# A state-space mixer on one core: chunk output, gate and skip term with channels on the partitions

## What is computed

```
gate, xbc, dt = split(h @ W_in.T)                 # 4096, 4096 + 2*1024, 64
x, B, C = split(silu(causal_conv4(xbc) + conv_b))
dt = softplus(dt + dt_bias);  A_cs = cumsum(dt * -exp(A_log)) within a chunk
Y_diag = ((C @ B.T) * exp(A_cs[l] - A_cs[s]), s <= l) @ (x * dt)
state  = decayed sum over chunks of B.T @ (x * dt * decay)
Y_off  = (C @ state_before) * exp(A_cs)
y   = Y_diag + Y_off + D * x
g   = y * silu(gate)
g   = g * rsqrt(mean over the 512 channels of a group (g*g) + eps) * norm_weight
out = g @ W_out.T
```

## Time and profile before

| | us |
|---|---|
| median of three runs (2715.51 to 2718.09) | 2717.3 |
| span of the profiled execution | 2716.7 |
| busy in it: TensorE matmul / VectorE / ScalarE / GpSimd | 2384.9 / 2075.4 / 1173.9 / 1157.6 |
| mixer's chunk loop, first to last output projection | 297 to 1616 |

### The profile page before, as it was taken

The page is one execution under the profiler, slowest core; times in us unless marked ns, Lnnn a source line. Parts: engine busy times, 40 slices in busy tenths (PEclk is TensorE's granted clock), DMA queues, the critical chain, the costliest instruction groups (busy, mean ns, idle before and its releaser), DMA issues. The chain is left out here.

```text
span 2716.7 us, 41390 instructions
## 1 busy us (share of the span) xinstructions
PE 2384.9 (88%) x14084; PEld 1851.0 (68%) x14084; DVE 2075.4 (76%) x3420; ACT 1173.9 (43%) x2311; POOL 1157.6 (43%) x1249
## 2 busy tenths in 40 slices
PE   4994999999999999999999972799999976888872
PEld 3784788888888888888888851688888864333322
DVE  5876888888888888888888856677777767766635
ACT  1431555555555555555555531122222223554551
POOL 3442565656656566565665540345555420000000
PEclk9996999999999999999999995899999997999996
DMA  2002000000000000000000010100000003111103
GB/s 84 1 13 96 3 3 30 3 29 4 3 30 3 30 3 3 30 3 30 3 3 3 3 57 7 33 26 26 26 26 20 26 20 108 52 50 49 51 34 122
DMA packets 72016, 77.75 MB, mean 29 GB/s; under 512 B 21120, under 2 KB 57312, under 8 KB 70560
## 3 DMA queue, kind: packets, MB, share of 16 engines
q1 hardware_dynamic: 71840, 75.51, 8.5%
HBM read 59.42 MB, written 15.86 MB: 28 GB/s over the span
## 5 line engine op out<-in xcount | busy, mean ns | idle before, releaser
L1043 DVE SCALAR_TENSOR_TENSOR mix_cv<-mix_pp,mix_cw,mix_cv 128x384 f32<-128x384 f32 (+4 forms) x864 | 493.1, 571 | 25.3 <-ACT mix_cv L966 4.5
L890 PEld LDWEIGHTS mix_pyd<-mix_xdt,mix_lm 128*128 128x128 f32 x2048 | 248.7, 193 | 56.7 <-issue 53.1
L1726 DVE TENSOR_REDUCE att_tops<-att_psc 128x1 f32<-128x512 f32 (+3 forms) x384 | 193.7, 552 | 104.9 <-PE att_psc L1677 72.0
L966 ACT ACTIVATE mix_cv<-mix_pp,mix_cb,mix_cw 128x384 f32<-128x384 f32 (+1 forms) x288 | 182.1, 632 | 210.7 <-PE mix_pp L77 210.7
L75 PE MATMUL mix_pp<-l0in_XH,mix_wx_lo 128*128 128x384 f32 (+2 forms) x576 | 239.0, 415 | 38.1 <-DVE mix_ss L1032 23.1
L829 POOL TENSOR_TENSOR mix_xdt<-mix_xtok,l_dt 128x512 f32<-128x512 f32 x128 | 133.5, 1043 | 279.2 <-ACT mix_xtok L993 279.2
L1202 POOL TENSOR_TENSOR ffn_hl<-ffn_h,ffn_hh 128x512 fp32r<-128x512 f32 x112 | 144.3, 1289 | 251.5 <-ACT ffn_hh L1260 251.5
L941 PE MATMUL mix_pgt<-mix_wo,mix_gt 128*128 128x256 f32 x1024 | 246.6, 384 | 2.9 <-issue 2.2
L890 PE MATMUL mix_pyd<-mix_xdt,mix_lm 128*128 128x64 f32 x2048 | 244.0, 273 | 2.6 <-DVE mix_lm L1093 2.6
L822 POOL TENSOR_TENSOR mix_t<-mix_t,mix_xd 128x512 f32<-128x512 f32 x112 | 144.3, 1288 | 219.6 <-DVE mix_t L1057 128.6
L1750 ACT ACTIVATE att_pr<-att_pst 128x1024 f32<-128x1024 f32 (+7 forms) x256 | 157.8, 651 | 153.9 <-PE att_pst L1688 79.5
(11 more groups left out here) (337 smaller groups left out, 6723.9 us busy)
## 6 DMA issues: line engine op xcount, KB each, us to landing
mix_w_raw<-in_w_in SPq DMA_DIRECT2D x8, 1280.0 KB, 5.7
ffn_raw<-in_wgu SPq DMA_DIRECT2D x56, 128.0 KB, 2.2
mix_ll<-cs SPq DMA_DIRECT2D x384, 4.0 KB
a_part<-att_sums SPq DMA_DIRECT2D x128, 34.0 KB
mix_wo_raw<-in_w_out SPq DMA_DIRECT2D x8, 512.0 KB, 6.7
ffn_draw<-in_wd SPq DMA_DIRECT2D x28, 128.0 KB, 2.1
q<-qkv_part SPq DMA_DIRECT2D x24, 128.0 KB, 1.9
k<-qkv_part SPq DMA_DIRECT2D x24, 128.0 KB, 1.9
```

Source lines behind the costliest of these rows:

```text
L890: last = pe.matmul(pyd[:, h * HP:(h + 1) * HP], lm[p % 2][:, h, :], xdt[p % 2][:, h * HP:(h + 1) * HP], start=True, stop=True)
L966: act.activation(conv_tile(k), pp[k % 2][:, halo:cols], ACT.Identity, bias=cb[:, it // 2, ct:ct + 1], scale=cw[:, it // 2, ct, 3:4]).then_ ...
L1043: last = dve.scalar_tensor_tensor(out, of, cw[:, g, ct, 3 - d:4 - d], out, ALU.mult, ALU.add)
L1726: dve.tensor_reduce(tops[o][:, col:col + 1], psc[PLACE[n, g] % RING][:, 0:end - c], AX.X, ALU.max).then_inc(mx_done, 1)
```

## The change

The chunk output is computed transposed. For each pair of heads, one head's 64 channels go to partitions 0 to 63 of the bank `py` and the other's to 64 to 127. The factor exp(A_cs), which varies along the tokens and so no longer lies on the partitions, comes from DRAM: `prelude` stores it, SyncE loads it for every chunk broadcast over the partitions (512 KB), and GpSimd multiplies it by C (`ce`). The state's part is then accumulated in PSUM by TensorE. The gate is projected with channels on the partitions, two channel tiles for two chunks at a time, one chunk ahead, and kept in SBUF (`sg`). D x is made by ScalarE from `cv` in four pieces. The result z is the stationary operand of the output projection as it stands; the four transposes and their copy go. The sum of squares over the partitions is two GpSimd adds and a matmul with a column of ones. The orders of all four engines change with it. SyncE's order for a chunk becomes: the weights of the next group (now after waits for the old group's last use; W_out goes straight into `wo`), the four decay rows as before, and for seven chunks in eight, after a wait for the head matmuls of c - 2, the load of `ce`.

```diff
 # TensorE, slot c
-if 0 <= p < NC and p % CPS: matmul(pyos, cv[:, CT_C, cols_of(p)], carry)
+def head_out(h): return py[h % 2 * HP:(h % 2 + 1) * HP, h // 2 * Q:(h // 2 + 1) * Q]
 if 0 <= p < NC:
+    wait u_done, carry_done, ce_done
     wait m_done, xdt_done
-    for h in range(GH): matmul(pyd[:, h*HP:(h+1)*HP], lm[:, h, :], xdt[:, h*HP:(h+1)*HP])
+    for k in range(NX):
+        if p % CPS:
+            for h in (2*k, 2*k+1): matmul(head_out(h), carry[:, h*HP:(h+1)*HP], ce[:, h, :], start=True, stop=False)
+        for h in (2*k, 2*k+1): matmul(head_out(h), xdt[:, h*HP:(h+1)*HP], lm[:, h, :], start=p % CPS == 0, stop=True)
 if ks: fill(ks[0])
-gate of p: 2 x matmul3(pgt, XH, XL, wg_hi, wg_lo)        # 6 matmuls of 512 columns
 if live:
+    wait(pe, acc_done, e + 1)                             # px holds e's projection
     transposes of x; transpose of B; scores
     decays(c, 0)
+if 0 <= c + 1 < NC: gate(c + 1)                           # 12 matmuls of 256 columns
+if live: decays(c, 1)
 if len(ks) > 2: fill(ks[1])
 state(p)
 if len(ks) > 1: fill(ks[-1])
-if live: decays(c, 1)
-projection of e
-four transposes of z of p
+wait zs_done;  matmul(px[:, D:D+1], zs, one)
+wait z_done;   projection of p, z as the stationary operand

 # ScalarE, slot c
-copy of transposed z (e)
 if len(fills(c-1)) > 1: squash(fills(c-1)[-1])
+if 0 <= e < NC: wait op_done, e + 1;  ss = px[:, D:D+1] + eps      # then GpSimd: rs = ss ** -0.5
 if ks: init(ks[0])
-tanh of the gate (p)
+if 0 <= p < NC: wait z_done;  zsq = square(z)
 if live: xtok = copy; btok = copy
 if ks: squash(ks[0])
 if live: exp of decay half 0
+if 0 <= c + 1 < NC: tanh of the gate (c + 1)
+if live: exp of decay half 1
 if len(ks) > 2: init(ks[1])
-if live: exp of decay half 1
-square of z with row sum (p)
+if live: for k in range(NX): xd[:, k, :] = cv[:, k, cols_of(c)] * dsk
 if len(ks) > 2: squash(ks[1])
 if len(ks) > 1: init(ks[-1])

 # VectorE, slot c
-t1 = pyos * exp_cs
 if len(fills(c-1)) > 1: finish(fills(c-1)[-1])
+if 0 <= e < NC: wait op_done, rs_done;  ACC += px * rs    # acc
-y = pyd + t1
+if 0 <= p < NC: u = py + xd;  z = u * sg
 if ks: taps(ks[0])
-w = (tanh + 1) * gate;  z = y * w
+if 0 <= c + 1 < NC: wait tg_done;  sg = (tanh + 1) * gate # w
 if ks: finish(ks[0])
-if len(ks) > 2: taps(ks[1])
-carry
 if live: lm = lm * scores
+if len(ks) > 2: taps(ks[1])
+carry
 if len(ks) > 2: finish(ks[1])
 if len(ks) > 1: taps(ks[-1])
-ACC += pgt * rs

 # GpSimd, slot c
-t1 += xd;  split piece
+rs = ss ** -0.5 (e)
+ce = ce * C (c);  zt, zs = sums of zsq (p)
 xdt; xdtd
-xd = xtok * D
+split piece
 decayed carry
-rs = (ss + eps) ** -0.5 (p)
```

More of the change, by code:

```diff
@@ L270, in _ @@
                     sp.dma_start(aneg[i * H0:(i + 1) * H0, :], a_log.rearrange("(h o) -> h o", o=1)).then_inc(dec_ld, 16)
+                sp.wait_ge(ax_done, 1)
+                for row in range(2):
+                    sp.dma_start(ecs_d[:, row * HT:(row + 1) * HT], e[row * H0:(row + 1) * H0, :]).then_inc(ecs_out, 16)
                 for i in range(3):
@@ L652, with mixer @@
 KD_ROWS = KM + HQ
[L655 to L656 removed]
+def mixer(nc, w_in, conv_w, conv_b, d_skip, norm_w, w_out, XH, XL, cs3, ecs_d, sel_rows, one_rows,
+          ident, TDT, TDTD, DCH, ACC):
     NC = G0 * 2 * CPS
@@ L832, in _ @@
                             pool.tensor_tensor(by_head(xdtd[o]), by_head(xtok[o]), heads(TDTD, c), ALU.mult).then_inc(xdtd_done, 1)
[L833 to L845, removed]
-                        pool.tensor_tensor(rs[o][:, :], rs[o][:, :], half[:, :], ALU.pow).then_inc(rs_done, 1)
+                    if live and 4 <= c % 16 < 13 and c // 16 < G0 - 1:
+                        split(c // 16 + 1, c % 16 - 4)
+                    if live and 0 < c % CPS < CPS - 1:
+                        pool.wait_ge(carry_done, n_off(c))
+                        pool.tensor_tensor(by_head(decayed), by_head(carry), heads(DCH, c), ALU.mult).then_inc(cd_done, 1)
             @block.tensor
@@ L920, in _ @@
                         decays(c, 0)
+                    if 0 <= c + 1 < NC:
+                        gate(c + 1)
+                    if live:
+                        decays(c, 1)
                     if len(ks) > 2:
@@ L1077, in _ @@
                     if ks:
                         finish(ks[0])
-                    if len(ks) > 2:
-                        taps(ks[1])
-                    if 0 <= p < NC and p % CPS < CPS - 1:
-                        dve.wait_ge(s_done, n_state(p))
-                        if p % CPS:
-                            dve.wait_ge(cd_done, n_decayed(p))
-                            dve.tensor_tensor(carry[:, :], decayed[:, :], pyos[:, :], ALU.add).then_inc(carry_done, 1)
-                        else:
-                            wait(dve, yo_done, n_off(p))
-                            wait(dve, cd_done, n_decayed(p))
-                            dve.tensor_copy(carry[:, :], pyos[:, :]).then_inc(carry_done, 1)
@@ L1095, in _ @@
                     if len(ks) > 2:
+                        taps(ks[1])
+                    if 0 <= p < NC and p % CPS < CPS - 1:
+                        dve.wait_ge(s_done, n_state(p))
+                        wait(dve, cd_done, n_decayed(p))
+                        if p % CPS:
+                            dve.tensor_tensor(carry[:, :], decayed[:, :], ps[:, :], ALU.add).then_inc(carry_done, 1)
+                        else:
+                            dve.tensor_copy(carry[:, :], ps[:, :]).then_inc(carry_done, 1)
+                    if len(ks) > 2:
                         finish(ks[1])
```

323 lines of the change are left out of this document (171 added, 152 removed).

## The result

| | before | after |
|---|---|---|
| median of the runs, us | 2716.4 (2714.4 to 2718.1) | 2951.8 (2949.8 to 2957.0) |
| span of the profiled execution | 2716.7 | 2949.5 |
| ratio of times | | 1.087 [1.085, 1.089] |

The change costs 235 us. The forecast was 2847, + 130 us, with 2780 to 2930 as its range: the sign is right, the size is not, and the time lies above the range.

A forecast was written before the change was run, and what follows sets the result against it. TensorE was taken to bound the kernel at 10.39 us a slot; after the change VectorE's work and waits would make 11.4, +1.02 x 128 = +130 us, so 2716.7 + 130 = 2847 us, range 2780 to 2930.

The forecast's parts named there:

- The load of ce is issued a slot ahead: SyncE's load of the decay factors for GpSimd's product: issued over 10 us ahead, so counted as nothing.
- Costs of the others stay: VectorE's remaining operations in a slot keep their times, z at 0.61 us; work 9.4 - 0.6 = 8.8 us.
- VectorE's waits, 1.67 + 0.64 + 0.28: Three new VectorE waits per wide slot: w for tanh 1.67 us, finish for squash 0.64, acc for the norm factor 0.28.
- (b): VectorE's last taps are followed at once by the same fill's finish, which waits for its squash: 0.64 us a slot.
- (c): VectorE's acc waits for the norm factor, from ss on ScalarE and then GpSimd's power: 0.28 us a slot.
- TensorE no longer the bound: TensorE waits some 1.7 us in every slot for the first exponential before its second decay half.
- The heads in 1.9 us, side by side: TensorE's 16 head products, two instructions each, run two at a time on different partition halves: 1.9 us a slot.
- rival 2: TensorE's heads don't run side by side: +154 us, 3001 us; chance 0.13 shared with Rival 4 and everything over 2900.
- Rival 1: TensorE stays the bound, VectorE's waits partly hidden: 2603 us; chance 0.08, including anything between it and no change.
- Rival 4: TensorE gets a lower clock in part of the loop: about 2950 us; chance 0.13 shared with rival 2 and everything over 2900.
- What would show it wrong: List of profile signs against the forecast, among them waits for ce or its load, which were held to be free.

The follow-up runs named there:

- z_psum_late: The changed kernel, load still in 512 B pieces, with VectorE's sum u written back into PSUM so z has one PSUM operand; 2895.6 us.
- ce4k: The changed kernel with the decay factors stored by chunk, so the load of ce comes in 128 pieces of 4 KB instead of 1024 of 512 B; 2996.4 us.
- z_psum: ce4k with VectorE's sum u written back into its PSUM bank, so z has one PSUM operand, and TensorE's next heads wait for z; 2834.6 us.
- act: z_psum with ScalarE's order changed: first exponential and tanh ahead of the squash of the first fill; 2732.3 us.
- both_row: z_psum_both with heads in the order 0, 2, 4, 6, 1, 3, 5, 7, so neighbours write the same half of the partitions; 2787.0 us.
- z_psum_both: act, plus ScalarE's ss ahead of the last squash and VectorE's acc ahead of the last finish; 2661.6 us, ratio 0.980.
- heads_row: ce4k with heads in an order in which neighbours write the same half of the partitions; 2992.6 us.
- ce4k_act: ce4k with ScalarE's first exponential and tanh put ahead of the squash of the first fill; 2837.4 us.

## Why the prediction was wrong, step by step

The kernels form a square; each entry is the median in us.

| | `ce` meets z | it can't hold z |
|---|---|---|
| load in 512 B pieces, late | 2951.8 (after) | 2895.6 (z_psum_late) |
| load in 4 KB pieces, in time | 2996.4 (ce4k) | 2834.6 (z_psum) |

Against the kernel before, the lower right is + 118 us: that is the change with only the waits that were forecast (+ 130). The late load adds 61, the hold on z another 56 on top of it: 118 + 61 + 56 = 235. The 56 are also what z's mean length gives, (1.128 - 0.692) x 128 = 56. The two are not independent. With the load in time the hold costs 162, because every `ce` then meets z; with it late many miss. That is why a repair of the load alone made the kernel slower.

- **"The load of ce is issued a slot ahead, over 10 us. Here I count nothing."** Wrong: this is the first step that failed. It was priced by the time available (some 10 us; for the load issued at 1071.58, GpSimd came to its product 9.35 us later, at 1080.93) and never by what the transfer needs: 1024 pieces of 512 B landed in a median of 14.2 us, the same bytes in 4 KB pieces in 3.6. It costs 61 us.
- **"Costs of the others stay: ... z 0.61."** Wrong: the second step that failed. y x gate had an operand in PSUM, z has none, and at the same point GpSimd gets an operation twice as long. Each was priced alone, from rows where the other did not exist. It costs 56 us here and would cost 162.
- **VectorE's waits, 1.67 + 0.64 + 0.28.** Right: 1.56, 0.56, 0.32, and a wide slot of 11.34 us against 11.4. Removing most of them by order gave 102 us (act) and 71 (acc) in z_psum; (b) and (c) were not taken apart.
- **TensorE no longer the bound, its gain spent in waiting 1.7 us for the first exponential.** Right: 1.49 in the slot shown.
- **The heads in 1.9 us, side by side (rival 2 at 3.6).** Right: 1.9. In a row they take 3.2, where rival 2 had 3.6. What rival 2 said it would cost, 154 us, is 125 between both_row and z_psum_both, where TensorE is near the bound and z isn't held; heads_row can't tell, since other things moved with it. The rule of the Trainium skill quoted against it, page "TensorE: Matmul & The Clock Gate", section "The mechanism", does not hold for these 64-column operands: all of them use all rows, and 32 were done in 1.9 us with their loads.
- **Rival 1, TensorE bound, 2603.** Wrong for this kernel, but it says what the rest costs: with both losses repaired and two reorderings it is 2662.
- **Rival 4, a lower clock in part of the loop.** Partly right: 0.97 in after. It was expected from TensorE idle in some 17% of each slot; z_psum is at 1.00 with TensorE 85% busy, and the falls in ce4k stand behind single waits of about 2 to 2.5 us. What it costs in after was not measured apart.
- **What would show it wrong** named "waits for ce or its load". That was the first row of the page after, so the doubt had been seen; it had no price and no place in the range.

## What to carry to other kernels

Price a load by its pieces and not by the time it may take, and ask what a queue holds behind the instruction that waits for it. When a change moves an operand from PSUM to SBUF, or gives GpSimd a long operation, look at which VectorE instructions with two SBUF operands run beside GpSimd: they may last until it is done. A run whose time doesn't move can hide a loss beside a gain (heads_row): look at the rows before calling it free. And undo suspects in pairs: here the repair of one loss alone (the load) made things worse, since it had been hiding the other.

## What the runs showed of the hardware

- A VectorE product with both operands in SBUF that began while a GpSimd product of 2.38 us ran ended 0.54 to 0.56 us after that one, and took mostly 1.67 us and up to 2.84 instead of 0.69; with one operand in PSUM it was not held. Where the VectorE product began first, it took 0.69 and the GpSimd product up to 2.66 us.
- A broadcast load of 512 KB took 14.2 us in pieces of 512 B and 3.6 in pieces of 4 KB.
- Head matmuls with 64-column stationary operands whose neighbours write different halves of the partitions run side by side: 32 in 1.9 us against 3.2.
- TensorE's granted clock fell to 0.50 behind some of the waits of 2.3 to 2.5 us in ce4k, not behind others, and stayed at 1.00 between 600 and 1500 us in z_psum, where none was over 1.7; in ce4k_act it fell to 0.53 behind one of 1.74.
